# All attention scores issued 1.6 places sooner, with eighteen probability tiles instead of fourteen

## The chip, the cores and the metric

The kernel runs on one core of a Trainium2 chip. The metric is the device time of one execution in microseconds (us), the median of the runs. The engines are TensorE (PE, with its weight loads shown as PEld), VectorE (DVE), ScalarE (ACT), GpSimd (POOL) and SyncE (SP, which here only issues DMAs). Each engine works through its own list of instructions in order; semaphores tie the lists together.

## The reference

One transformer layer over 2 x 1024 tokens of width 512, in FP32, with 16 heads of 32:

```python
qkv = einsum('bsd,ed->bse', x, w_qkv) + b_qkv             # split into q, k, v, 16 heads
scores = q @ k^T / sqrt(32) + causal mask
attn = softmax(scores); out = attn @ v
x = layernorm(x + out @ w_out^T + b_out)
hidden = relu((x @ sign(up_w)^T) * up_scale)
x = layernorm(x + (hidden @ sign(down_w)^T) * down_scale * output_scale)
```

## The kernel before

Matmuls that need more precision than one pass gives are split into a high and a low part (`x_high`, `x_low` and so on). The order of all work is one list, made by `plan()` (L86): every piece of work is put at a *slot*, a number, and the list is sorted by slot, ties by the order of the calls. Every engine's block then walks this same list and issues what concerns it. So a slot decides only what stands before what, on each engine; it is no time.

Attention runs in 8 steps (`STEPS`), one for a batch element and a group of four heads. Step s covers the slots from 48s to 48s+48. Inside a step there are 48 *scores* (`NP`, L29): score n belongs to one half f of the queries (f=0 for n below 16), one tile j of 128 keys and one of the four heads h. A score is one matmul on PE (L1013), 512, 384, 256 or 256 columns wide for j on the diagonal (the last, 128 wide, is issued 256 wide) and 512 for the others. ACT takes its exponential out of PSUM into one of `RING` tiles of `probs` (L709), POOL masks the diagonal ones (L617). Score n of a step stands at slot n (L142).

What else stands in a step:

- `pv` (L1043) multiplies the four heads' probabilities of one tile j by v into `ps_heads`, `sum` (L1037) adds them up with ones into `ps_sum`. In steps 0 to 5 these groups go in pairs: groups 0 and 1 at slot 13, 2 and 3 at 19.6, 4 and 5 at 28, 6 and 7 at 36, 8 and 9 at 44, 10 and 11 at 52 (which is slot 4 of the next step), by `PAIRED` (L35). Steps 6 and 7 take them one by one (`ALONE`, L37). For groups 4 to 7 POOL first adds probabilities (L630), and `sum_added` (L1021, slot 43.9) sums those.
- `norm` (L824): after groups 0 to 3 (f=0), and again after 4 to 11 (f=1), DVE reads both banks, four times a reciprocal and a product into `heads_sb` (L833, L835). The next `pv` with j=0 waits for all four (L1028), since it writes into the same bank.
- `max` (L981, slots in `MAXIMA`, L42): 48 *units* of the next step's scores, whose row maxima DVE takes (L807, L811), and which become the shift of its softmax: `shift` (L992, ACT L694, DVE L821), at slots 36.02 and 51.9.
- `proj` (L945, slots in `BLOCK`, L46): the projections of q and k of later steps, with their evictions `full` and `high` on ACT (L682, L688).
- In step 6 `sign` and `split` on ACT and DVE (L715 to L745, L840) prepare late weights and fetched heads; in step 7 `attn` (L1061) is the output projection of the first 512 tokens, `std1` (L748) and `norm1` (L873) its layernorm, `turn` (L1070) its transposes. The FFN begins at slot 384.5 (`FIRST_UP`, L70; L1085, L1102).

Scores, units and shifts share five PSUM banks (four for the scores of step 7) in rotation, by `share()` (L229): each takes the bank used longest ago, and its matmul waits until ACT or DVE has read what lies there (`bank_read`, L916). An exponential also waits until the tile that it overwrites, `RING` scores back, was used (L705 to L708). Before the attention the `probs` tiles hold the first pieces of x (L444, L453).

Of the kernel before, what the change touches and what calls it, by code (L numbers as in the profile page):

```python
# [18 lines left out]
GH = P // HD  # L19
# [7 lines left out]

PIECES = [(f, j, h) for f in range(2) for j in range(4 * (f + 1)) for h in range(GH)]
NP = len(PIECES)  # L29
RING = 14  # L30
DIAG = [n for n, (f, j, h) in enumerate(PIECES) if j >= 4 * f]
ND = len(DIAG)


PAIRED = [13, 13, 19.6, 19.6, 28, 28, 36, 36, 44, 44, 52, 52]  # L35
# [16 lines left out]
FIRST_ADD, LAST_ADD = 4, 8  # L52
NA = 3 * GH
ADDING = STEPS - 2
# [31 lines left out]
def plan():  # L86
# [4 lines left out]
    def put(slot, what, s=0, n=0):  # L91
        todo.append((slot, len(todo), (what, s, n)))
# [39 lines left out]
        put(at + 6.5, "keep", 1, k)  # L132
        put((-104.5, -97)[k], "stack", 1, k)
    put(-104, "v_rows", 0)
    put(-1, "ones", 1)
    put(0.9, "row_max", 0, 1)
    put(1.2, "shift", 0, 1)

    for s in range(STEPS):
        t = NP * s  # L140
        for n in range(NP):
            put(t + n, "score", s, n)  # L142
        paired = s < STEPS - 2
        for g, at in enumerate(PAIRED if paired else ALONE[s % 2]):
            put(t + at, "pv", s, g)
            if g < FIRST_ADD or g >= LAST_ADD or s >= ADDING:
                put(t + at, "sum", s, g)
        if s < ADDING:
            for a in range(NA):
                put(t + 21.7 + 1.3 * a, "add", s, a)  # L150
            put(t + 43.9, "sum_added", s)
        for q, at in enumerate(PAIRED_NORM if paired else ALONE_NORM[s % 2]):
            put(t + at, "norm", s, q)
            if q % 4 == 3:
                put(t + at + 4.9, "store", s, q // 4)
        if s + 1 < STEPS:
            for u, at in enumerate(MAXIMA):
                put(t + at, "max", s + 1, u)
            put(t + 36.02, "shift", s + 1, 0)
            put(t + 47.2, "row_max", s + 1, 1)  # L160
            put(t + (51.9 if s + 2 < STEPS else 48.2), "shift", s + 1, 1)
            put(t + 17, "v_rows", s + 1)
        for ahead, k, at, each, evict, keep, fill in BLOCK if s < STEPS - 2 else LAST_BLOCK:
            if s + ahead < STEPS:
                for m in range(12):
                    put(t + at + each * m, "proj", s + ahead, 12 * k + m)
                put(t + evict, "full", s + ahead, k)
                put(t + evict + 0.05, "high", s + ahead, k)
                put(t + keep, "keep", s + ahead, k)
                put(t + fill, "stack", s + ahead, k)  # L170
# [30 lines left out]
    for i in range(CH):  # L201
        t = FIRST_UP + 16 * i
# [47 lines left out]
def build(nc, x_rows, x_cols, w_qk, w_v, b_qk, b_v, w_out, b_out, up_w, down_w, up_s, down_s, out_s, out):  # L250
    top = ExitStack()
    with top:
# [404 lines left out]
        def _(act):  # L657
# [4 lines left out]
            for what, s, n in todo:  # L662
# [33 lines left out]
                if what == "score":  # L696
                    _, width, _ = piece_cols(n)
                    off = P if width == P else 0
                    if s == 0 and n == 0:

                        act.wait_ge(s_xl[0], 8)
                        act.wait_ge(s_xl[1], 8)
                    act.wait_ge(s_score, NP * s + n + 1)

                    wait(act, s_pv, NP * s + n - RING + 1)  # L705
                    k = n - RING - GH * FIRST_ADD
                    if s < ADDING and 0 <= k < GH * (LAST_ADD - FIRST_ADD):
                        act.wait_ge(s_add, NA * s + (k if k < GH else k - GH) + 1)  # L708
                    nc.scalar.activation(probs[:, (NP * s + n) % RING, 0:width], bank(what, s, n)[:, off:off + width],  # L709
                                         ACT.Exp, scale=SCALE).then_inc(s_exp, 1)  # L710
                if what == "sign":
                    act.wait_ge(s_raw[n % 2], 16 * (n // 2 + 1))
                    src = raw[:, n % 2, :]
                    if n < 2:
                        nc.scalar.activation(wo[0][:, 2 * n:2 * n + 2, :].rearrange("p c e -> p (c e)"), src,  # L715
                                             ACT.Copy).then_inc(s_sign, 1)
                    elif n < 10:
                        if n == 6:

                            act.wait_ge(s_score, NP * (STEPS - 1))  # L720
                        k = (n - 2) % 4
                        nc.scalar.activation(up_sb[(n - 2) // 4][:, 2 * k:2 * k + 2, :, :].rearrange("p m c e -> p (m c e)"),
                                             src, ACT.Sign).then_inc(s_sign, 1)
                    else:
                        if n == 14:

                            act.wait_ge(s_pv, NP * STEPS)
                            act.wait_ge(s_st[1], 16 * STEPS)
                        if n == 10:

                            for k in range(NB):
                                act.wait_ge(s_stack[k], 48 * STEPS)
                            act.wait_ge(s_lo, NB * STEPS)
                        nc.scalar.activation(down_sb[:, 2 * (17 - n):2 * (18 - n), :].rearrange("p m e -> p (m e)"),
                                             src, ACT.Sign).then_inc(s_sign, 1)
# [416 lines left out]
```

## Time and profile before

| | us |
|---|---|
| median of 3 runs | 782.07 (779.53 to 782.5) |
| the profiled execution | 783.35, its span 781.6 |
| PE busy | 730.8 (94%) |
| DVE, ACT, POOL busy | 450.3, 317.0, 354.9 |
| mean granted TensorE clock | 0.979 |
| DMA queues | q1 and q10 hardware_dynamic, q8 and q14 instruction; no other |

PE is busy nearly throughout, so what can move is the little time in which it waits, and the stretches in which its clock is granted at half. The timeline rows read: start in us, duration in us, engine, line, operation, tiles written and read, partitions and columns, and how many instructions are merged (x). In brackets stands how long the engine was idle before, and what released it. Matmuls are pipelined: the distance from one start to the next is what one costs, and it is shorter than its duration.

### The profile page before, as it was taken

To read this page: it belongs to the slowest core of one execution; us is meant where nothing else is said; L and a number is where in the kernel's file an instruction comes from. 1 tells how busy PE (TensorE), PEld (TensorE's weight loads), DVE (VectorE), ACT (ScalarE), POOL (GpSimd) and SP (SyncE) were. 2 spreads that over 40 slices of the span, in tenths; PEclk is the share of its full clock that TensorE was granted. 3 is DMA by queue.
4 is the path that set the end of the run, shared out by engine and by line. 5 is a ranking of instruction groups with operands and counts; after the bars stand their busy time and mean duration, and the time that the engine had idled before them with its cause. 6 is when DMAs were issued, how large, how long until landed. Compare 5 with 4: busy or idle time off the path is not lost.

```text
span 781.6 us, 11689 instructions
## 1 busy us (share of the span) xinstructions
PE 730.8 (94%) x4032; PEld 508.9 (65%) x4032; DVE 450.3 (58%) x1086; ACT 317.0 (41%) x631; POOL 354.9 (45%) x487
## 2 busy tenths in 40 slices
PE   6899999999999999999978989999999999999993
PEld 4688665655656556565534543788778787878882
DVE  4176496785957859578566651632295429434515
ACT  5211355554655546565446556423222222221210
POOL 4461467394674947648322501542344235323333
PEclk9999999999999999999989899999999999999997
DMA  6965454435545354442577240403003101000101
GB/s 228 297 188 146 127 178 133 137 109 149 161 135 145 91 161 139 129 143 83 152 225 243 83 136 27 149 28 122 14 28 107 24 5 41 15 1 0 55 1 54
DMA packets 44619, 85.71 MB, mean 110 GB/s; under 512 B 4880, under 2 KB 13584, under 8 KB 44432
## 3 DMA queue, kind: packets, MB, share of 16 engines
q1 hardware_dynamic: 35536, 79.72, 33.8%
q10 hardware_dynamic: 9024, 5.24, 2.4%
q8 instruction: 32, 0.52, 0.3%
q14 instruction: 27, 0.22, 0.1%
HBM read 55.33 MB, written 29.36 MB: 108 GB/s over the span
## 4 chain that ended last, share of the span: by engine, by line
PE 70%; DVE 20%; issue 3%; DMA 3%; ACT 2%; POOL 1%; SPq 0%; ACTq 0%; DVEq 0%; POOLq 0%
PE ps_heads L1043 9%; PE ps_proj L1085 7%; DVE heads_sb L833 7%; PE ps_proj L945 6%; PE ps_score L1102 6%; PE ps_unit L1061 6%; DVE maxes L811 6%; PE ps_sum L1037 6%; PE ps_unit L1085 5%; PE ps_unit L981 4%; PE ps_heads L1102 3%; PE ps_sum L1102 3%; PE ps_unit L1013 3%; DVE heads_sb L835 2%; PE ps_score L981 2%
## 5 line engine op out<-in xcount | busy, mean ns | idle before, releaser
L653 POOL TENSOR_TENSOR hid_low<-hid_raw,hid_high 128x512 fp32r<-128x512 f32 x64 | 85.0, 1329 | 175.2 <-DVE hid_high L884 172.1
L709 ACT ACTIVATE probs<-ps_unit 128x512 f32<-128x512 f32 (+3 forms) x215 | 101.1, 491 | 91.7 <-PE ps_unit L1013 87.9
L617 POOL TENSOR_SCALAR_AFFINE_SELECT probs<-probs 128x128 f32<-128x128 f32 x256 | 73.3, 296 | 129.6 <-ACT probs L709 125.1
L709 ACT ACTIVATE probs<-ps_score 128x512 f32<-128x512 f32 (+3 forms) x156 | 75.1, 496 | 76.2 <-PE ps_score L1013 73.8
L807 DVE CUSTOM_DVE_ANT_0 ps_unit<-ps_unit,causal 128x256 f32<-128x256 f32 (+3 forms) x164 | 80.4, 509 | 41.2 <-PE ps_unit L981 40.3
L884 DVE CAST hid_high<-hid_raw 128x512 fp32r<-128x512 f32 x64 | 27.1, 424 | 127.2 <-ACT hid_raw L764 126.9
L981 PE MATMUL ps_unit<-stack 96*128 96x512 f32 (+3 forms) x247 | 86.0, 363 | 7.6 <-DVE maxes L807 3.8
L1043 PE MATMUL ps_heads<-probs,v_rows 128*32 128x512 f32 (+3 forms) x768 | 81.9, 504 | 10.1 <-DVE heads_sb L835 10.1
L1013 PE MATMUL ps_unit<-stack 98*128 98x512 f32 (+2 forms) x215 | 77.8, 368 | 3.9 <-DVE maxes L807 3.9
L611 POOL TENSOR_TENSOR parts<-qk_full,parts 128x512 fp32r<-128x512 f32 x32 | 41.1, 1284 | 58.2 <-ACT parts L688 58.0
L981 PEld LDWEIGHTS ps_unit<-stack 96*128 96x128 f32 x247 | 46.7, 193 | 31.6 <-DVE maxes L811 10.9
L833 DVE RECIPROCAL heads_sb<-ps_sum 128x128 f32<-128x128 f32 x64 | 60.8, 950 | 11.0 <-PE ps_sum L1037 11.0
L811 DVE TENSOR_REDUCE maxes<-ps_unit 128x1 f32<-128x512 f32 x83 | 54.3, 683 | 17.9 <-PE ps_unit L981 17.8
L630 POOL TENSOR_TENSOR added<-added,probs 128x512 f32<-128x512 f32 x48 | 60.9, 1282 | 0.0
L764 ACT ACTIVATE hid_raw<-ps_proj,up_scale 128x512 f32<-128x512 f32 x32 | 22.0, 689 | 93.6 <-PE ps_proj L1085 93.6
L1013 PE MATMUL ps_score<-stack 98*128 98x512 f32 (+2 forms) x156 | 57.2, 373 | 2.6 <-DVE h_even L789 1.5
L807 DVE CUSTOM_DVE_ANT_0 ps_score<-ps_score,causal 128x512 f32<-128x512 f32 (+3 forms) x92 | 46.1, 517 | 23.1 <-PE ps_score L981 22.8
L1037 PE MATMUL ps_sum<-probs,ones 128*32 128x512 f32 (+3 forms) x576 | 57.8, 467 | 0.0
L1013 PEld LDWEIGHTS ps_unit<-stack 98*128 98x128 f32 x215 | 41.0, 191 | 17.7 <-DVE maxes L807 4.3
L945 PE MATMUL ps_proj<-x_high,w_high 128*128 128x512 f32 x116 | 45.9, 422 | 6.7 <-ACT x_high L666 6.7
L1102 PE MATMUL ps_score<-down_sb,hid_high 128*128 128x512 f32 x124 | 50.1, 404 | 0.0
L981 PE MATMUL ps_score<-stack 96*128 96x512 f32 (+3 forms) x137 | 47.7, 362 | 1.6 <-DVE maxes L807 1.1
(195 smaller groups left out, 1456.7 us busy)
## 6 DMA issues: line engine op xcount, KB each, us to landing
stack<-qk_parts SPq DMA_DIRECT2D x96, 256.0 KB, 4.5
qk_parts<-parts SPq DMA_DIRECT2D x32, 512.0 KB, 2.8
v_all<-h_even ACTq DMA_DIRECT2D x16, 256.0 KB, 3.3
v_rows<-v_all SPq DMA_DIRECT2D x8, 512.0 KB, 4.6
heads_t<-heads_sb SPq DMA_DIRECT2D x16, 256.0 KB, 3.1
raw<-up_w SPq DMA_DIRECT2D x8, 512.0 KB, 3.5
x_tile<-x_rows SPq DMA_DIRECT2D x16, 256.0 KB, 5.0
raw<-down_w SPq DMA_DIRECT2D x8, 512.0 KB, 3.9
```

The lines of the kernel that those rows point to most:

```text
L653: nc.gpsimd.tensor_tensor(hid[1][:, (HM * s + n) % 3, :], hid_raw[:, n % 2, :], hid[0][:, (HM * s + n) % 3, :].bitcast(FP32), ALU.subtract ...
L709: nc.scalar.activation(probs[:, (NP * s + n) % RING, 0:width], bank(what, s, n)[:, off:off + width], ACT.Exp, scale=SCALE).then_inc(s_exp, 1)
L807: nc.vector.tensor_tensor_reduce(bank(what, s, n)[:, 0:width], bank(what, s, n)[:, 0:width], causal[:, HALF - width:], 1.0, NEG, ALU.add, ...
L811: nc.vector.tensor_reduce(maxes[:, 1, col:col + 1], bank(what, s, n)[:, :], AXIS_X, ALU.max).then_inc(s_max, 1)
L833: nc.vector.reciprocal(heads_sb[:, cols], ps_sum[:, cols]).then_inc(s_rc, 1)
L945: mm = nc.tensor.matmul(proj_bank(s, k)[:, :], ws[wp][:, c, t, :], xs[xp][:, c, t0:t0 + HALF], start=(m == 0), stop=(m == 11))
L981: nc.tensor.matmul(bank(what, s, n)[:, 0:width], stack[s % 2][0:96, 1, f, h, i % 4 * P:(i % 4 + 1) * P], stack[s % 2][0:96, 0, c, h, 0:wid ...
L1013: nc.tensor.matmul(bank(what, s, n)[:, 0:width + off], stack[s % 2][0:98, 0, j // 4, h, j % 4 * P:(j % 4 + 1) * P], stack[s % 2][0:98, 1, ...
L1037: nc.tensor.matmul(ps_sum[rows, at:at + width], ones[:, :], tile, **args).then_inc(s_pv, 1)
L1043: mm = nc.tensor.matmul(ps_heads[rows, at:at + width], v_rows[:, s % 2, j, rows], tile, **args)
L1085: mm = nc.tensor.matmul(ps_up[n % 2][:, :], up_sb[n // 8][:, n % 8, m % DC, :], turned[s % 2][m // DC][:, m % DC, :], start=(m == 0), stop ...
L1102: mm = nc.tensor.matmul(ps_down[i][:, :], hid[part][:, (HM * s + n) % 3, i * P:(i + 1) * P], down_sb[:, down_at(n), :], start=(n == 0 and ...
```

## The change

Three things. The scores (and with them their exponentials and masks, which are issued at the same entry of the list) are put at slot n - 1.6 instead of n; nothing else is moved except `ones` of step 1, which has to stay ahead. The ring of `probs` grows from 14 to 18 tiles. The room for it (4 x 2 KB a partition) comes from the scratch memory of software-driven DMAs, cut to 1024 bytes, which also lets two more of the late weights' pieces be written before the last probabilities are used (`n == 16`). The wait of an exponential for POOL's additions is written so that it also holds across steps.

```diff
-RING = 14
+RING = 18
+LEAD = 1.6
...
-    put(-1, "ones", 1)
+    put(-1 - LEAD, "ones", 1)
...
         for n in range(NP):
-            put(t + n, "score", s, n)
+            put(t + n - LEAD, "score", s, n)
...
                     wait(act, s_pv, NP * s + n - RING + 1)
-                    k = n - RING - GH * FIRST_ADD
-                    if s < ADDING and 0 <= k < GH * (LAST_ADD - FIRST_ADD):
-                        act.wait_ge(s_add, NA * s + (k if k < GH else k - GH) + 1)
+                    s0, k = (NP * s + n - RING) // NP, (n - RING) % NP - GH * FIRST_ADD
+                    if 0 <= s0 < ADDING and 0 <= k < GH * (LAST_ADD - FIRST_ADD):
+                        act.wait_ge(s_add, NA * s0 + (k if k < GH else k - GH) + 1)
...
-                        if n == 14:
+                        if n == 16:
...
-    nc = bacc.Bacc("TRN2", target_bir_lowering=False, num_devices=1)
+    nc = bacc.Bacc("TRN2", target_bir_lowering=False, num_devices=1, dynamic_dma_scratch_size=1024)
```

Below, lines of the changed kernel are two higher than those of before (from L135 on).

**PE, across the end of step 1.** These are the last groups of step 1 (L1043 and L1037, 256 and 128 columns), and the scores of step 2 around them (L1013, 384 columns wide for n = 4 to 7), with projections (L945) between. Before:

```order
L992 MATMUL ps_unit<-ident,row_max 16x128
L1043 MATMUL ps_heads<-probs,v_rows 32x256 x4
L1037 MATMUL ps_sum<-probs,ones 32x256 x4
L1043 MATMUL ps_heads<-probs,v_rows 32x128 x4
L1037 MATMUL ps_sum<-probs,ones 32x128 x4
L1013 MATMUL ps_unit<-stack 128x384
L945 MATMUL ps_proj<-x_low,w_high 128x512
L1013 MATMUL ps_unit<-stack 128x384
L945 MATMUL ps_proj<-x_low,w_high 128x512
L1013 MATMUL ps_score<-stack 128x384
L945 MATMUL ps_proj<-x_low,w_high 128x512
L1013 MATMUL ps_score<-stack 128x384
```

After:

```order
L1015 MATMUL ps_unit<-stack 128x384
L947 MATMUL ps_proj<-x_high,w_high 128x512
L1015 MATMUL ps_unit<-stack 128x384
L947 MATMUL ps_proj<-x_high,w_high 128x512
L994 MATMUL ps_unit<-ident,row_max 16x128
L1045 MATMUL ps_heads<-probs,v_rows 32x256 x4
L1039 MATMUL ps_sum<-probs,ones 32x256 x4
L1045 MATMUL ps_heads<-probs,v_rows 32x128 x4
L1039 MATMUL ps_sum<-probs,ones 32x128 x4
L1015 MATMUL ps_score<-stack 128x384
L947 MATMUL ps_proj<-x_low,w_high 128x512
L1015 MATMUL ps_score<-stack 128x384
```

Before, the four scores of 384 columns all follow the groups; after, two of them stand ahead of the groups and of the shift (L992, L994 after), and two behind. Between these groups and the next (slot 13) PE has 10 scores before and 9 after, beside the same units and projections. From the groups at slot 19.6 to those at 28 it has 9 before and 8 after.

**PE, at slot 43.9 of step 1.** L1021 is the sum of the added tiles, L1043 the first group of the pair at 44, L1013 a score. Before:

```order
L1013 MATMUL ps_unit<-stack 128x256
L981 MATMUL ps_unit<-stack 128x384
L1021 MATMUL ps_sum<-added,ones 32x512 x4
L1013 MATMUL ps_unit<-stack 128x256
L1043 MATMUL ps_heads<-probs,v_rows 32x512 x4
L1037 MATMUL ps_sum<-probs,ones 32x512 x4
```

After:

```order
L1015 MATMUL ps_unit<-stack 128x256
L983 MATMUL ps_score<-stack 128x384
L1023 MATMUL ps_sum<-added,ones 32x512 x4
L1045 MATMUL ps_heads<-probs,v_rows 32x512 x4
L1039 MATMUL ps_sum<-probs,ones 32x512 x4
```

The lone score between the sum and the pair has moved ahead of both.

**ACT, at slot 22.5 of step 7.** The table loads stand around the standard deviation (L748, L750 after), the exponentials are L709 (L711 after), L754 (L756 after) copies the first transpose. The tile names are the banks in their rotation of four. Before:

```order
L709 ACTIVATE probs<-ps_unit2 128x512
L709 ACTIVATE probs<-ps_score0 128x512
L748 ACT_TABLE_LOAD
L748 ACTIVATE std1<-mom1,eps 128x4
L709 ACT_TABLE_LOAD
L709 ACTIVATE probs<-ps_proj 128x512
L709 ACTIVATE probs<-ps_score1 128x512
L709 ACTIVATE probs<-ps_unit2 128x512
L709 ACTIVATE probs<-ps_score0 128x512
L754 ACTIVATE t_even_high<-ps_unit1 128x4x128
```

After:

```order
L711 ACTIVATE probs<-ps_proj 128x512
L711 ACTIVATE probs<-ps_score0 128x512
L750 ACT_TABLE_LOAD
L750 ACTIVATE std1<-mom1,eps 128x4
L711 ACT_TABLE_LOAD
L711 ACTIVATE probs<-ps_score1 128x512
L711 ACTIVATE probs<-ps_unit2 128x512
L711 ACTIVATE probs<-ps_proj 128x512
L756 ACTIVATE t_even_high<-ps_unit1 128x4x128
```

Before, scores 23 to 26 follow the table loads and the copy of the first transpose comes behind four of them; after, scores 23 and 24 are done ahead, and the copy comes behind three (25 to 27).

## Rows read from the trace of the kernel before

**Rows 1.** windows view (busy time by stretch); columns in its first line

```profile
core 0: us, PE busy (x) PEld busy (x) DVE busy (x) ACT busy (x) POOL busy (x), PEclk, DMA share, GB/s
88.50:401.00 312.50, 296.93 (x2011) 185.97 (x2011) 224.04 (x634) 173.05 (x375) 190.66 (x319) 1.00 0.48 138
401.00:489.40 88.40, 78.55 (x476) 38.35 (x476) 42.52 (x97) 51.53 (x99) 23.70 (x53) 0.90 0.40 126
```

**Rows 2.** the same view, around the stretches at the lower clock

```profile
397.80:401.20 3.40, 0.15 (x1) 0.00 (x0) 3.30 (x7) 1.04 (x2) 0.24 (x1) 1.00 0.67 271
401.20:408.00 6.80, 6.16 (x21) 2.22 (x22) 1.23 (x5) 2.69 (x5) 2.35 (x1) 0.50 0.64 154
435.40:442.20 6.80, 6.38 (x35) 3.67 (x27) 1.26 (x5) 2.94 (x6) 3.60 (x7) 0.50 0.02 5
466.10:469.50 3.40, 1.43 (x7) 0.79 (x6) 1.64 (x4) 3.36 (x7) 0.00 (x0) 1.00 0.00 0
469.50:472.90 3.40, 3.40 (x17) 0.60 (x16) 1.15 (x2) 2.06 (x5) 0.00 (x0) 0.50 0.00 0
```

**Rows 3.** line 1043 (heads matmuls), idle before it: us, times

```profile
  DVE heads_sb L835: 24.4, 26
  POOL probs L617: 3.5, 9
```

**Rows 4.** timeline of PE around two waits for the normalization (before and in step 3)

```profile
238.54 0.28 PE L1013 MATMUL ps_score<-stack 98*128 98x256 f32 x1
239.76 0.64 PE L1043 MATMUL ps_heads<-probs,v_rows 128*32 128x512 f32 x4 [0.95 <-DVE heads_sb L835]
...
254.76 0.40 PE L945 MATMUL ps_proj<-x_low,w_high 128*128 128x512 f32 x1
255.00 0.39 PE L1013 MATMUL ps_unit<-stack 98*128 98x512 f32 x1
255.81 0.64 PE L1043 MATMUL ps_heads<-probs,v_rows 128*32 128x512 f32 x4 [0.42 <-DVE heads_sb L835]
```

**Rows 5.** timeline of DVE, first and last of one normalization

```profile
234.86 0.96 DVE L833 RECIPROCAL heads_sb<-ps_sum 128x128 f32<-128x128 f32 x1 [0.75 <-PE ps_sum L1037]
...
239.41 0.29 DVE L835 TENSOR_TENSOR heads_sb<-ps_heads,heads_sb 128x128 f32<-128x128 f32 x1
```

**Rows 6.** timeline of PE around the sum of the added tiles (step 2)

```profile
224.13 0.28 PE L1013 MATMUL ps_unit<-stack 98*128 98x256 f32 x1
224.25 0.34 PE L981 MATMUL ps_unit<-stack 96*128 96x384 f32 x1
...
225.51 0.38 PE L1013 MATMUL ps_score<-stack 98*128 98x256 f32 x1
225.83 0.64 PE L1043 MATMUL ps_heads<-probs,v_rows 128*32 128x512 f32 x4
```

**Rows 7.** timeline of PE, step 6, after the first normalization

```profile
401.84 1.65 PE L1013 MATMUL ps_unit<-stack 98*128 98x512 f32 x3 [3.88 <-DVE maxes L807]
```

**Rows 8.** timeline of ACT, DVE and PE, step 6, the second split

```profile
427.32 0.62 ACT L745 ACTIVATE t_even_high<-h_even 128x512 fp32r<-128x512 f32 x1
427.98 0.69 DVE L840 TENSOR_TENSOR t_even_low<-h_even,t_even_high 128x512 fp32r<-128x512 f32 x1 [0.89 <-ACT t_even_high L745]
...
429.13 0.33 PE L981 MATMUL ps_unit<-stack 96*128 96x128 f32 x1 [1.26 <-DVE maxes L807]
```

**Rows 9.** timeline of ACT and PE, step 7, after the standard deviation

```profile
466.73 1.28 ACT L709 ACT_TABLE_LOAD   x1
468.76 0.47 PE L1013 MATMUL ps_proj<-stack 98*128 98x512 f32 x1 [0.55 <-ACT probs L709]
469.62 1.08 PE L1043 MATMUL ps_heads<-probs,v_rows 128*32 128x512 f32 x4
```

**Rows 10.** timeline of PE, last score and first matmul of the FFN

```profile
488.65 0.38 PE L1013 MATMUL ps_proj<-stack 98*128 98x256 f32 x1
489.44 0.47 PE L1085 MATMUL ps_proj<-t_even_high,up_a 128*128 128x512 f32 x1 [0.41 <-issue]
```

## The prediction

> **What bounds the kernel now.** I read first the busy time by stretch: through steps 0 to 5 of the attention PE is busy 296.93 of 312.50 us at a full clock of 1.00, through the rest of the attention 78.55 of 88.40 at 0.90 [rows 1]. So PE bounds the kernel, and only its idle time and its clock can change, since the edit removes and adds no work. Then what PE's idle time ends on, line by line: before the heads matmuls it is 24.4 us in 26 entries (13 waits, each seen once by the matmuls and once by their weight loads) for the normalization on DVE, against 3.5 us for masked probabilities [rows 3]. The timeline gives one wait of each kind: 238.54 to 239.76 is 1.22 us for a score that costs 0.12, and 255.00 to 255.81 is 0.81 us for one that costs 0.24 [rows 4, 6]. One normalization takes DVE from 234.86 to 239.41 + 0.29 = 239.70, 4.84 us, whatever PE does beside it, and PE's next group starts 0.06 us after its end [rows 4, 5]. Last the clock by stretch: three pieces of 6.80, 6.80 and 3.40 us run at 0.50, that is 1.2 of 2.4 GHz, all in steps 6 and 7; ahead of the first PE was busy 0.15 of 3.40 us, ahead of the third 1.43 of 3.40 [rows 2].
>
> **The change, part by part.** Prices are start-to-start distances: 0.24 us for 512 columns (254.76 to 255.00, [rows 4]), 0.12 for 256 (224.13 to 224.25, [rows 6]), 0.18 for 384 between them.
>
> *The waits for the normalization, steps 0 to 5 and the starts of 6 and 7.* Between the groups that end a half and those that need `ps_heads` free, PE has scores, units and projections to do beside DVE's 4.84 us. After slot 52 it had scores 4 to 13 (four of 384 columns, six issued with 256), now 6 to 14: 0.18 + 0.18 - 0.12 = 0.24 us of cover less. From 19.6 to 28 it had nine of 512 columns, now eight: 0.24 less. The end of these stretches is set by DVE, so each becomes not shorter but idler, and the score that left is done where PE is busy: from 13 to 19.6 (scores 14 to 19 become 15 to 21) and from 44 to 52. There are six waits of the first kind that bind (before steps 1 to 6), six of the second, and one in step 7 from 17.5 to 24 (seven scores become six). 13 x 0.24 = **+3.1 us**.
>
> *From 28 to 36* DVE's row maxima pace PE; a score of 512 columns is replaced there by one of 384, which saves nothing, since DVE sets the end: 6 x 0.06 = **+0.3**.
>
> *The lone score at slot 43.9*, between the sum of the added tiles and the pair of groups, costs 225.51 to 225.83, 0.32 us, and 0.12 in a row of its like [rows 6]. It moves ahead of both: 6 x 0.20 = **-1.2**.
>
> *Step 6, normalization at 18.4.* Two units stand behind it on DVE, so PE runs out of banks for 3.88 us, then does three scores in 1.65 us before the next group [rows 7]. Afterwards it gets two scores further before it stops, and two instead of three follow the release. The group starts with the release of DVE plus two: **-0.5** (1.65/3 at the half clock, 0.24 at the full one).
>
> *Step 6, the second split.* ACT's half at 427.32 stands behind the exponential of score 40, which in turn waits for a matmul behind group 8 (slot 39.5). DVE's half waits 0.89 us for it, and PE then waits 1.26 us for a bank [rows 8]. Now scores 40 and 41 are ahead of the group. ACT still has a conversion of weights and two exponentials to do ahead, so I take only part of the 0.89: **-0.7**, between 0 and -1.26.
>
> *Step 7, the standard deviation.* ACT loads a table for the square root and one back (1.28 us, [rows 9]); the exponentials of 23 and 24 wait behind. PE therefore waits 0.55 us at 468.76 and does two scores before the group at 469.62. Now 23 and 24 are ahead of the tables, score 28 finds its bank free, and only 29 waits until about 468.76: the group starts one score sooner, **-0.4** (469.62 - 468.76, halved). Two turns later PE waits for ACT's and DVE's copies of a transpose, with two scores as cover in place of three: **+0.2**.
>
> *End of the attention.* The FFN's first matmul needs the bank of score 47, issued right before it: 488.65 to 489.44, 0.79 us where 0.12 are work [rows 10]. With score 47 ahead of group 10 its exponential is long done: **-0.7**.
>
> *What costs nothing.* The larger ring only takes a wait away: with 14 tiles, exponential 14 (now at slot 12.4) would need the tile that group 0 gives back at slot 13; with 18, number 18 does, at slot 16.4. ACT's evictions at 13.05, 19.65 and 44.05 now have one or two exponentials more ahead of them; the groups of heads and sums that stand there on PE cover that. If they did not, the projection behind would start up to 0.62 us later (a 512-column copy on ACT, [rows 8]), in stretches at whose end PE idles anyway. ACT's copy of the shift at 51.9 has two more exponentials ahead; the normalization behind it on DVE had been idle 0.75 us before its start [rows 5], and that takes it up. On SP no entry passes another; its DMAs for stacks and parts hang on units and projections, which keep their places. POOL's masks pass some additions of steps 0 to 5, whose sum is taken 8 slots after the last of them. The smaller scratch serves software-driven DMAs, and no queue here is one.
>
> Sum: 3.1 + 0.3 - 1.2 - 0.5 - 0.7 - 0.4 + 0.2 - 0.7 = **+0.1 us**. On the profiled execution's 783.35 that is 783.4; it stood 1.3 above the median, so I forecast 782.07 + 0.1 = 782.2.
>
> **What the clock does** is not in this sum, and its bounds are wide. In the three half-clock pieces PE is busy 6.16 + 6.38 + 3.40 = 15.94 us [rows 2]; if none came, 8.0 us would be saved. One more like the first would cost 6.16/2 = 3.1. I take no change, since the idle stretch of 3.88 us ahead of the first shrinks only to about 3.6.
>
> In steps 0 to 5 PE idles about 1.1 us at a time ([rows 4]: 1.22 - 0.12) and the clock stays at 1.00 [rows 1]. The Trainium skill, in "TensorE: Matmul & The Clock Gate", section "A second HAM failure mode: psum-queue depth-cycling", says that short idles between groups of matmuls that cycle through PSUM banks make the clock swing between its two levels, each swing costing throughput. This kernel is of that kind; its trace disagrees at 1.1 us of idleness, and at 3.88 us it agrees. By the rule the longer waits cost what rival 2 gives, by the rows nothing beyond the sum.
>
> **Rivals.**
> 1. *The clock stays up.* The change shortens the idleness ahead of the half-clock pieces: 0.55 us in step 7 [rows 2, 9], some 0.7 in step 6 a few us before 435.40 [rows 8]. If the last two pieces vanish: (6.38 + 3.40)/2 = 4.9 us, so 782.2 - 4.9 = 777.3; all three, 774.2. Against it: of the 3.40 - 1.43 = 1.97 us of idleness ahead of the third only 0.55 go.
> 2. *The clock falls in the early steps*, the slower side. The waits at a step's start grow from 1.1 to 1.34 us. If that is enough for a fall, each costs up to 3.1 us. From two on the kernel is slower: 782.2 + 6.2 = 788.4; with all six, about 801. Against it: rows at 1.00 throughout, and the step up is only 0.24.
> 3. *Only the lost cover shows.* The savings in steps 6 and 7 hang on chains over three engines; if they all come to nothing, 782.07 + 3.1 + 0.3 - 1.2 + 0.2 = 784.5, and without the lone score's 785.7.
> 4. *The lead does not arrive*: if PE's banks, not the order, hold the scores back, they are executed where they were, and the time is 782.1.
>
> **Chances.** Forecast 0.40, rival 1 0.20, rival 2 0.12, rival 3 0.18, rival 4 0.10. A measurement of this kernel can tell 0.5% from no change, 3.9 us. Faster than 778.2: rival 1, and 0.02 of the rest, 0.22. Slower than 786.0: rival 2, and 0.05 of rival 3 with a bad wait on top, 0.17. Same: 0.61. The forecast's own range is 780 to 784.5 from the bounds of the split and the step 6 terms; the range given, 776.8 to 786.8, takes in most of rivals 1 and 3 and leaves out the clock's far ends.
>
> **What would show it.** Right: the waits before the pair at slot 13 grow to about 1.46 us from the last score's start, those before slot 28 to 1.05; the distance from the pair at 13 to the pair at 28 grows from 16.05 us (239.76 to 255.81, [rows 4]) by 0.34, the score and a half more ahead of slot 19.6; no score stands between the sum and the pair at 44; the FFN's first matmul follows without an idle. Wrong: if steps 1 to 5 get shorter, the stretches that I took as paced by PE had slack; if the granted clock of steps 6 and 7 is far from 0.90, the time is the clock's and not the sum's.

## The result, and the profile after

The changed kernel takes 775.69 us (median of 19 runs, 773.07 to 779.61), the kernel before 780.25 (19 runs on the same chips, 777.48 to 782.5). The ratio is 0.9947, with a 95% interval of 0.9934 to 0.996: 4.1 us faster. The forecast was 782.2, no change, with a range of 776.8 to 786.8. It stood on 782.07, the median of three runs; the nineteen give 780.25, so 1.8 us of the distance are the base's and not the change's. The profiled execution took 774.34 us, its span is 772.6 (before 781.6), at a mean granted clock of 0.991 (before 0.979).

The page of the changed kernel, span and busy times, then the clock in 40 slices (tenths of 2.4 GHz):

```profile
span 772.6 us, 11683 instructions
...
PE 722.7 (94%) x4032; PEld 505.2 (65%) x4032; DVE 450.5 (58%) x1086; ACT 317.2 (41%) x631; POOL 354.4 (46%) x487
...
PEclk9999999999999999999999999999999999999998
```

PE is busy 8.1 us less with the same 4032 matmuls: 722.7 against 730.8. Nearly all of it is clock: in the half-clock pieces of the two profiles (the one in the start-up, shown below, among them) PE is busy 22.26 us before and 6.66 after, and half of the difference is 7.8. Busy time by stretch, as in [rows 1], and then around the clock's steps, as in [rows 2]:

```profile
85.40:398.00 312.60, 296.55 (x2013) 186.32 (x2013) 223.34 (x633) 174.92 (x377) 190.27 (x319) 1.00 0.48 138
398.00:480.40 82.40, 72.96 (x474) 35.63 (x474) 43.35 (x99) 49.76 (x97) 23.33 (x53) 0.96 0.42 135
396.70:400.10 3.40, 0.32 (x1) 0.19 (x1) 3.33 (x8) 0.27 (x1) 0.00 (x0) 1.00 0.48 175
400.10:403.50 3.40, 3.26 (x14) 0.89 (x17) 0.28 (x2) 2.03 (x3) 1.55 (x1) 0.50 1.06 246
428.80:432.20 3.40, 2.35 (x20) 1.01 (x20) 2.32 (x11) 1.19 (x2) 1.58 (x3) 1.00 0.31 110
432.20:435.60 3.40, 3.26 (x28) 2.43 (x29) 1.00 (x3) 2.56 (x5) 3.31 (x5) 1.00 0.04 7
458.20:461.60 3.40, 1.76 (x8) 0.97 (x8) 1.64 (x4) 3.36 (x5) 0.00 (x0) 1.00 0.00 0
461.60:465.00 3.40, 3.40 (x17) 0.60 (x16) 1.15 (x2) 2.17 (x5) 0.00 (x0) 0.50 0.00 0
```

Steps 0 to 5 take about as long as before (312.60 us for 312.50, both at 1.00; from their first group to group 4 of step 6, 0.6 us more). Steps 6 and 7 take 82.40 for 88.40. The half-clock piece at 435.40 of [rows 2] has no counterpart: at 432.20 the clock stays at 1.00. The first piece is 3.40 us long instead of 6.80. The third is unchanged.

Part of the 9.0 us between the two spans is no gain of the change. The FFN begins 8.99 us earlier, but 2.8 of these are there already at the first group of step 0: before, the clock fell at 36.00 us in the start-up, behind this stretch of PE (kernel before, windows):

```profile
32.50:36.00 3.50, 1.45 (x7) 0.83 (x5) 0.00 (x0) 0.00 (x0) 1.12 (x1) 1.00 1.10 304
36.00:42.80 6.80, 6.32 (x16) 5.19 (x17) 2.99 (x10) 1.15 (x2) 2.52 (x2) 0.50 1.09 349
```

and after, it did not, behind nearly the same (the changed kernel):

```profile
32.50:36.00 3.50, 1.48 (x7) 0.86 (x5) 0.00 (x0) 0.00 (x0) 1.16 (x1) 1.00 1.08 308
36.00:42.80 6.80, 6.59 (x31) 5.56 (x32) 4.89 (x17) 2.31 (x4) 3.63 (x3) 1.00 1.09 346
```

Among the profiles of the kernels below whose start-up is that of before, three show such a piece, 3.4 us long (1, 6 and 7 of the list), and the others don't. The first group starts at 94.52 us in the profile of before, at 91.9 to 92.3 in those three and at 90.1 to 91.1 in the others. Two profiles, then, differ by 1 to 4 us that is chance. So I use two measures from here on: distances inside a profile for what the order does, and for the clock the half-clock time of a run, 2 x (1 - granted clock) x span, averaged over the runs of a kernel. It is 19.9 us for the changed kernel (13.9 to 28.0) and 27.5 to 29.8 for the kernel before in the different sets of runs. In every profile 7 to 9 us of it lie at the very end, where PE has no work left, so only the differences count. Among runs of one kernel, 1 us more of it goes with 0.33 to 0.39 us (before) or 0.35 us (after) more time; this is an association among runs, no experiment.

Where the order tells, by distances in the profiles (after less before): from the pair at slot 13 to that at 28 in step 3, +0.38; from the pair at 36 to that at 44, -0.30 to -0.38 in each early step; from 44 to the next 52, +0.04; all in all 0.6 us more from step 0 to step 5, about 0.1 a step. From group 4 of step 6 to the start of step 7, 39.18 us for 44.56: -5.4. From there to group 10 of step 7, -0.5, and from group 10 to the FFN, -0.9.

### The profile page after: what moved, and what is told of

Its sections match the earlier page's. It is cut to its first block, busy times and chain, and to the rows that moved or that the text cites. A ratio compares the mean times of both kernels' runs of the same rounds, so it can differ in the third digit from the quotient of the medians.

```text
span 772.6 us, 11683 instructions
## 1 busy us (share of the span) xinstructions
PE 722.7 (94%) x4032; PEld 505.2 (65%) x4032; DVE 450.5 (58%) x1086; ACT 317.2 (41%) x631; POOL 354.4 (46%) x487
## 4 chain that ended last, share of the span: by engine, by line
PE 71%; DVE 19%; issue 3%; DMA 3%; POOL 2%; ACT 2%; SPq 0%; ACTq 0%; POOLq 0%
PE ps_heads L1045 9%; PE ps_proj L1087 7%; DVE heads_sb L835 7%; PE ps_proj L947 7%; PE ps_score L1104 6%; PE ps_unit L1063 6%; PE ps_unit L1087 5%; PE ps_sum L1039 5%; DVE maxes L813 5%; PE ps_unit L983 4%; PE ps_heads L1104 3%; PE ps_unit L1015 3%; PE ps_sum L1104 3%; PE ps_score L1015 2%; PE ps_score L983 2%
## 5 line engine op out<-in xcount | busy, mean ns | idle before, releaser
L711 ACT ACTIVATE probs<-ps_unit 128x512 f32<-128x512 f32 (+3 forms) x216 | 101.9, 490 | 88.4 <-PE ps_unit L1015 85.0
L711 ACT ACTIVATE probs<-ps_score 128x512 f32<-128x512 f32 (+3 forms) x155 | 75.2, 498 | 77.0 <-PE ps_score L1015 75.6
L809 DVE CUSTOM_DVE_ANT_0 ps_unit<-ps_unit,causal 128x512 f32<-128x512 f32 (+3 forms) x162 | 80.1, 511 | 32.5 <-PE ps_unit L983 31.5
L1045 PE MATMUL ps_heads<-probs,v_rows 128*32 128x512 f32 (+3 forms) x768 | 80.3, 502 | 11.8 <-DVE heads_sb L837 11.8
L983 PE MATMUL ps_unit<-stack 96*128 96x512 f32 (+3 forms) x246 | 83.8, 354 | 5.7 <-DVE maxes L809 2.5
L1039 PE MATMUL ps_sum<-probs,ones 128*32 128x512 f32 (+3 forms) x576 | 55.5, 457 | 0.0
L1045 PEld LDWEIGHTS ps_heads<-probs,v_rows 128*32 128x32 f32 x768 | 19.5, 109 | 47.8 <-issue 23.6
```

What stands on the lines that cost most here:

```text
L809: nc.vector.tensor_tensor_reduce(bank(what, s, n)[:, 0:width], bank(what, s, n)[:, 0:width], causal[:, HALF - width:], 1.0, NEG, ALU.add, ...
L983: nc.tensor.matmul(bank(what, s, n)[:, 0:width], stack[s % 2][0:96, 1, f, h, i % 4 * P:(i % 4 + 1) * P], stack[s % 2][0:96, 0, c, h, 0:wid ...
L1039: nc.tensor.matmul(ps_sum[rows, at:at + width], ones[:, :], tile, **args).then_inc(s_pv, 1)
L1045: mm = nc.tensor.matmul(ps_heads[rows, at:at + width], v_rows[:, s % 2, j, rows], tile, **args)
```

## The experiments

Three explanations stood against each other: the clock (less idleness in step 6, so less time at half clock; the lead's own waits about nothing), the waits (the edit's savings are larger than priced, wherever they lie, at the same clock), and the ring of 18 tiles with its smaller scratch. Each kernel was timed against the kernel before on the same chip, in three sets: kernels 1 to 4 in one, 5, 6, 7 and 9 in the next, 8 and 10 to 12 in the last. The half-clock time of the kernel before is 27.5, 28.1 and 29.8 us in these sets. Half-clock time is the mean per run, as defined above. Where a difference of two ratios is given, "give or take" comes from their two intervals.

| | median, us (runs) | ratio to before, 95% | half-clock, us |
|---|---|---|---|
| changed kernel | 775.69 (19) | 0.9947 [0.9934, 0.9960] | 19.9 |
| 1. ring alone | 780.63 (12) | 1.0008 [0.9993, 1.0022] | 30.0 |
| 2. lead in steps 0 to 5 | 782.37 (12) | 1.0028 [1.0009, 1.0046] | 28.9 |
| 3. lead in steps 6 and 7 | 774.66 (6) | 0.9933 [0.9914, 0.9952] | 18.6 |
| 4. lead in step 7 | 779.50 (12) | 0.9986 [0.9972, 1.0000] | 27.9 |
| 5. lead in step 6 | 776.49 (7) | 0.9951 [0.9933, 0.9969] | 20.8 |
| 6. before + fillers | 777.09 (7) | 0.9955 [0.9939, 0.9971] | 14.6 |
| 7. steps 6, 7 + fillers | 775.04 (6) | 0.9916 [0.9889, 0.9942] | 13.9 |
| 8. changed + fillers | 773.93 (6) | 0.9903 [0.9875, 0.9930] | 13.4 |
| 9. split moved | 778.76 (12) | 0.9983 [0.9971, 0.9996] | 26.2 |
| 10. lone score moved | 779.03 (12) | 0.9981 [0.9963, 0.9999] | 28.9 |
| 11. steps 6, 7 + lone score | 772.08 (6) | 0.9890 [0.9856, 0.9925] | 17.5 |
| 12. all of it | 769.82 (6) | 0.9854 [0.9828, 0.9881] | 10.5 |

**1. The ring alone.** The changed kernel, with the lead at 0:

```diff
+LEADS = [0.0] * 8
...
-            put(t + n - LEAD, "score", s, n)
+            put(t + n - LEADS[s], "score", s, n)
```

> Ring of 18, small scratch, but every score at its old slot (lead 0): the order on every engine is that of before. Theory A (the order of the scores makes the gain): same time as before, ratio 0.999 to 1.001, and the first half-clock stretch at 36 us comes and goes as in before. Rival (the ring or the moved buffers make part of the gain, at the start, where the changed kernel's profile reaches the first score 3.1 us sooner): ratio 0.996 to 0.997.

1.0008 [0.9993, 1.0022]: the ring and the smaller scratch show no gain by themselves (by the interval at most 0.6 us). The gain is the order's.

**2. The lead in steps 0 to 5 only.** `LEADS = [LEAD] * 6 + [0.0] * 2`.

> The lead of 1.6 in steps 0 to 5 only, steps 6 and 7 at their old slots. Theory A (gain sits in steps 6 and 7; early steps cost 0.1 us each): ratio 1.000 to 1.002, the start of group 4 of step 5 0.6 us later than before once the start-up is taken off. Rival (the early steps or the start-up gain): ratio below 0.998.

1.0028 [1.0009, 1.0046], 2.2 us slower (0.7 to 3.6), more than expected. The early part costs, as the waits for the normalization said it would.

**3. The lead in steps 6 and 7 only**, rising over the first two scores of step 6:

```diff
+            put(t + n - (0 if s < 6 else min(LEAD, 0.8 * n) if s == 6 else LEAD), "score", s, n)
```

> The lead in steps 6 and 7 only. Theory A: the whole gain or a little more, ratio 0.993 to 0.995 (4 to 5 us), with fewer or shorter half-clock stretches between 400 and 475 us. Rival (gain is in the early part): ratio above 0.998.

0.9933 [0.9914, 0.9952], as expected: the whole gain, and the half-clock time goes from 27.5 to 18.6 us. So it lies late.

**4. The lead in step 7 only** (the same line with 7 for 6).

> The lead in step 7 only. Theory A with the sizes of the two profiles (step 6, from group 4 to the next step's group 0, gave 5.4 us of which much is clock; step 7 from group 4 on 1.7): ratio 0.998 (1.1 to 1.7 us faster). Rival (step 7 carries the gain): ratio 0.995.

0.9986 [0.9972, 1.0000], 1.1 us, at an unchanged half-clock time (27.9 for 27.5).

**5. The lead in step 6 only** (rising at its start, falling again over the first scores of step 7).

> The lead in step 6 only, taken back over the first scores of step 7. From the lead in 6 and 7 (0.9933) and in 7 alone (0.9986): ratio 0.994 to 0.996 if the two add up; half-clock time a run 7 to 9 us less than before. My sum had 1.2 us for step 6 at an unchanged clock: 0.9985 if the clock played no part.

0.9951 [0.9933, 0.9969], as expected: 3.8 us of the gain come with step 6, and with them the clock (20.8 us for 28.1).

**6. Fillers in the kernel before.** The order is the one of before. Added are 24 matmuls of 512 columns whose result is thrown away, into `ps_proj`, which is free there: 14 where PE runs out of banks [rows 7], and 5 twice near the second split [rows 8].

```diff
+        for at, count in [(21.5, 14), (42.05, 5), (46.04, 5)]:
+            for m in range(count):
+                put(late + at, "fill", 0, m)
...
+                if what == "fill":
+                    pe.wait_ge(s_qk, NB * STEPS)
+                    nc.tensor.matmul(ps_proj[:, :], stack[0][0:98, 0, 0, 0, 0:P], stack[0][0:98, 1, 0, 0, :], start=True, stop=True)
```

> The kernel before with 24 matmuls of 512 columns added in step 6, into the idle ps_proj bank, whose results are thrown away: 14 where PE waits 3.88 us for DVE behind the normalization, 5 and 5 where it waits 1.26 and 1.2 us for a bank. Theory C (part of the gain is clock: idle PE ahead of 401 and 435 us gives the half-clock stretches): both stretches vanish, half-clock time a run falls by 8 to 13 us, ratio 0.994 to 0.996. Rival W (only the waits count, the clock is an accident beside it): the waits' ends stay where DVE and ACT set them, and the added work costs or changes nothing, ratio 1.000 to 1.002.

0.9955 [0.9939, 0.9971], as theory C expected: 3.5 us faster with more work and nothing else. The timeline of PE of this kernel, where [rows 7] have 3.88 us of idleness and three scores in 1.65 us (L1116 are the fillers, L1016 scores):

```profile
395.06 3.36 PE L1116 MATMUL ps_proj<-stack 98*128 98x512 f32 x14
399.12 1.15 PE L1016 MATMUL ps_unit<-stack 98*128 98x512 f32 x3 [0.70 <-DVE maxes L810]
400.20 1.07 PE L1046 MATMUL ps_heads<-probs,v_rows 128*32 128x512 f32 x8
```

From the first of the three scores to the group are 1.08 us now, 1.58 before (401.84 to 403.42), and the windows of the same kernel show why, and that of the pieces in steps 6 and 7 only the last is left:

```profile
395.00:398.40 3.40, 3.40 (x15) 2.47 (x14) 3.30 (x6) 1.09 (x2) 0.32 (x1) 1.00 0.67 271
398.40:401.80 3.40, 2.70 (x20) 0.90 (x19) 1.31 (x5) 2.14 (x4) 0.04 (x1) 1.00 0.75 174
435.40:442.00 6.60, 6.60 (x49) 5.01 (x42) 5.94 (x10) 5.44 (x11) 4.62 (x11) 1.00 0.38 121
463.40:466.80 3.40, 3.40 (x19) 1.04 (x12) 1.14 (x2) 1.53 (x4) 0.00 (x0) 0.50 0.00 0
```

The half-clock time falls by 13.5 us (28.1 to 14.6), the time by 3.5, or 0.26 us for each. In "TensorE: Matmul & The Clock Gate", section "HAM oscillation — how this bites in real kernels", the Trainium skill counts half of the throttled time as lost. Here it is less. That a slow PE runs into waits that it would have had anyway would explain it, but no run here separates that.

**7. Fillers in kernel 3**: 13 at slot 22.0 and 5 at 45.6 of step 6.

> The lead in steps 6 and 7 only (774.7 us, 0.9933), and 18 such matmuls: 13 in the wait behind step 6's normalization, 5 in the one before group 10. Theory C: 1 to 2 us faster than with the lead alone, ratio 0.990 to 0.992, no half-clock stretch at 397 to 401 us. Rival W: ratio 0.993 to 0.995.

0.9916 [0.9889, 0.9942]: inside the expected ratio, but 1.3 us below kernel 3, give or take 2.5, so the clock's part in kernel 3 does not stand out of the noise. Its profile still has a half-clock piece of 3.4 us behind the fillers, at 401.6, where theory C expected none; the half-clock time is 13.9 us, near kernel 6's 14.6. At this level of the clock, kernel 6's mean of 776.93 us becomes 773.79: 3.1 us, give or take 2.4, are the late lead's own.

**8. Fillers in the changed kernel**, the same 18.

> The changed kernel with 18 thrown-away matmuls in step 6, as in the kernel with the late lead (0.9916). The difference between the two is the price of the lead in steps 0 to 5 with the clock of step 6 levelled. By my sum's waits and the traces' other terms 0.6 to 2 us: ratio 0.9925 to 0.9945. Rival (the early lead costs nothing): 0.9916 again.

0.9903 [0.9875, 0.9930], faster than expected; the rival's 0.9916 lies inside the interval. Against kernel 7, from which it differs only by the lead of steps 0 to 5 (and the chip), it is 1.0 us faster, give or take 3.0: too wide to contradict kernel 2, which had that lead cost 2.2 us (0.7 to 3.6). The traces have a price too: 0.6 us from the first group on, and the first group itself starts at 91.7 to 91.8 us in the three profiles with the early lead (changed, 2, 8), at 90.1 to 91.1 in the seven that have neither it nor the piece in the start-up, about 1.1 us more.

This kernel against kernel 6 is the whole change with fillers on both sides: 0.9903 for 0.9955, 4.1 us, give or take 2.5, at nearly the same half-clock time (13.4 and 14.6). The change gains as much between these two as without fillers.

**9. The second split alone**, ahead of the group in the kernel before:

```diff
-        put(late + 38 + 2 * i, "split", 0, i)
+        put(late + (39.49 if i == 1 else 38 + 2 * i), "split", 0, i)
```

> The kernel before, but ACT's half of the second split (slot 40) stands ahead of the exponential of score 40, at 39.49; every score keeps its place. My term of the sum for it: 0.7 us, so ratio 0.9985 to 0.9995, DVE's wait of 0.89 us before its half gone. Rival (the clock amplifies it, since the idle ahead of the stretch at 435 us shrinks below what starts it): ratio 0.995 to 0.997 with that stretch gone. Rival (other waits take its place): 1.000.

0.9983 [0.9971, 0.9996], 1.3 us, where 0.7 was expected. DVE's half no longer waits, and of PE's 1.26 us [rows 8] stay 0.21 (timelines of DVE and PE):

```profile
423.02 0.69 DVE L840 TENSOR_TENSOR t_even_low<-h_even,t_even_high 128x512 fp32r<-128x512 f32 x1
...
424.17 0.33 PE L981 MATMUL ps_unit<-stack 96*128 96x128 f32 x1 [0.21 <-DVE maxes L807]
```

But the half-clock piece behind it stays. Windows of this kernel, then of kernels 5 and 3:

```profile
426.80:430.20 3.40, 2.09 (x16) 1.30 (x19) 2.85 (x10) 1.24 (x4) 2.31 (x4) 1.00 0.45 154
430.20:437.00 6.80, 6.38 (x35) 3.73 (x31) 1.50 (x6) 2.61 (x6) 3.38 (x7) 0.51 0.02 5
```

```profile
426.80:430.20 3.40, 2.26 (x21) 1.05 (x20) 2.72 (x11) 1.12 (x4) 1.30 (x5) 1.00 0.52 161
430.20:437.00 6.80, 4.70 (x34) 3.38 (x35) 3.95 (x7) 3.16 (x6) 5.49 (x7) 1.00 0.02 4
```

```profile
426.80:430.20 3.40, 2.09 (x20) 1.03 (x20) 2.62 (x11) 1.34 (x4) 1.30 (x4) 1.00 0.48 157
```

At 430.20 the clock is 0.51 in kernel 9 and 1.00 in kernel 5, and it stays up in kernel 3 too. PE's busy time ahead is 2.09 us in kernel 9, where it falls, and 2.26 and 2.09 where it doesn't: these rows do not tell which. What the runs say is that the split alone takes little half-clock time away (26.2 us for 28.1), and step 6's whole lead much (20.8).

**10. The lone score alone.** In the kernel before, score 44 of steps 0 to 5 ahead of the sum:

```diff
+            put(t + n - (0.15 if n == 44 and s < ADDING else 0), "score", s, n)
```

> The kernel before, with one edit: in steps 0 to 5 score 44 stands at 43.85, ahead of the sum of the added tiles (43.9), so that no lone score is left between that sum and the pair at 44. My price was 0.20 us a step; the two traces have 0.31 (8.76 us from the pair at 36 to the pair at 44 became 8.44). Expected 1.2 to 2.0 us less, ratio 0.9975 to 0.9985. Rival (the time is given back at the next wait): 1.000.

0.9981 [0.9963, 0.9999], 1.5 us, as expected. The timeline of PE in step 2, to be read against [rows 6] (their first entries are the same score and unit):

```profile
219.93 0.28 PE L1013 MATMUL ps_unit<-stack 98*128 98x256 f32 x1
220.05 0.34 PE L981 MATMUL ps_unit<-stack 96*128 96x384 f32 x1
220.23 0.28 PE L1013 MATMUL ps_score<-stack 98*128 98x256 f32 x1
220.44 1.07 PE L1021 MATMUL ps_sum<-added,ones 128*32 128x512 f32 x8
221.32 1.04 PE L1043 MATMUL ps_heads<-probs,v_rows 128*32 128x512 f32 x8
```

From the first score to the pair are 1.39 us, before 225.83 - 224.13 = 1.70: 0.31 a step. The score saves its 0.20, and the sum itself gets 0.1 shorter with the pair right behind it (0.88 from start to start).

**11. The late lead with the lone score** (kernels 3 and 10 together).

> The lead of 1.6 in steps 6 and 7 only (0.9933), and score 44 of steps 0 to 5 at 43.85. If the parts add up: 1.2 to 2.0 us below the late lead alone, ratio 0.991 to 0.992, and faster than the changed kernel (0.9947) by about 2 us. Rival (the early lead was worth its place): 0.994 or more.

0.9890 [0.9856, 0.9925]: faster than the changed kernel, whose interval begins at 0.9934, and a little more than the parts together. Its step 6 has the order of kernel 3, yet its profile shows a half-clock piece where those of kernels 3 and 5 have none:

```profile
423.40:426.80 3.40, 2.25 (x22) 1.10 (x21) 2.93 (x11) 1.41 (x4) 1.28 (x4) 0.99 0.49 161
426.80:433.60 6.80, 6.17 (x31) 3.67 (x28) 1.40 (x5) 3.00 (x5) 4.75 (x7) 0.50 0.01 2
```

PE was busy 2.25 us ahead of it, 2.26 in kernel 5, where the clock stays up. So in a single profile this piece is partly chance, and only the half-clock time of many runs tells (17.5 us here, for 29.8).

**12. All of it**: kernel 11, with 19 fillers in step 6 (14 at 22.0, 5 at 45.6) and 10 in step 7, into a bank free there:

```diff
+        for at, count in [(23.9, 5), (25.9, 5)]:
+            for m in range(count):
+                put(last + at, "fill", 1, m)
```

> Late lead, score 44 at 43.85, the 19 fillers of step 6, and 10 more in step 7 (five ahead of group 4, where PE waits 1.4 us for the normalization, five ahead of the first transpose, where it waits 1.4 us for the layernorm). Theory C: the half-clock stretch near 462 us goes too, ratio 0.986 to 0.989, the fastest. Rival W (idle time was free to fill, its clock worth nothing): as with the lead and score 44 alone, 0.991 to 0.992.

0.9854 [0.9828, 0.9881], 11.4 us faster than before, a little beyond the expected 0.986, and the fastest of all. Its window of steps 6 and 7:

```profile
395.00:474.00 79.00, 74.00 (x492) 38.63 (x494) 43.68 (x100) 49.25 (x95) 23.19 (x52) 1.00 0.43 138
```

They take 79.00 us at a clock of 1.00, where [rows 1] have 88.40 at 0.90. The half-clock piece of step 7 is gone, but the profiles of kernels 2 and 8 lack it too, without fillers there. The runs tell more: 10.5 us of half-clock time, of which 7 to 9 lie at the very end, for 17.5 in kernel 11.

## Why the prediction was wrong

The step that failed is the term of the clock: "I take no change, since the idle stretch of 3.88 us ahead of the first shrinks only to about 3.6." A run of the changed kernel has 19.9 us of half-clock time, one of the kernel before 27.5 to 29.8. The stretch itself did not even shrink. PE in step 6 of the changed kernel, as in [rows 7]:

```profile
395.20 0.62 PE L1015 MATMUL ps_unit<-stack 98*128 98x512 f32 x2
399.78 0.51 PE L1015 MATMUL ps_unit<-stack 98*128 98x512 f32 x1 [3.96 <-DVE maxes L809]
...
401.15 1.94 PE L1045 MATMUL ps_heads<-probs,v_rows 128*32 128x512 f32 x8
```

It idles 3.96 us and the clock still falls there, if for 3.40 us only. But the text argued from one of three pieces. The one at 435.40 goes, which was the core of rival 1, held at 0.20; the piece of step 7, which rival 1 counted on too, stays. The text also put all half-clock pieces of the trace into steps 6 and 7, and left out the one in the start-up. Its own sign of being wrong came true: the clock of steps 6 and 7 is 0.96 and not 0.90.

How much of the gain is clock, three readings tell. Over the runs, 7.6 to 9.9 us less half-clock time, at 0.35 each, would be 2.7 to 3.5 of the 4.1 us. The second reading is the stretch from group 4 of step 6 to group 0 of step 7, in the kernel before, the changed kernel, kernel 6 and kernel 8 (the kernel before and the changed one, with 24 and 18 fillers):

```profile
403.42:447.98 44.56, 40.08 (x220) 20.51 (x219) 26.02 (x64) 25.81 (x49) 17.65 (x32) 0.87 0.52 164
401.15:440.33 39.18, 36.29 (x220) 18.43 (x219) 25.86 (x64) 25.03 (x49) 17.77 (x33) 0.97 0.56 180
400.20:441.36 41.16, 37.47 (x230) 20.07 (x229) 27.08 (x64) 25.86 (x50) 17.60 (x32) 1.00 0.55 176
401.06:439.24 38.18, 36.10 (x226) 19.03 (x225) 25.87 (x64) 25.54 (x50) 17.76 (x33) 1.00 0.59 187
```

At full clock on both sides the stretch still gets 3.0 us shorter, so of the 5.4 us some 2.4 are clock and 3.0 the order's own, if the fillers themselves cost nothing. (Half of the difference in busy time at half clock, 12.54 us [rows 2] to 3.26, would make 4.6: too much.) The third are the times of kernels 8 and 6: with nearly the same half-clock time on both sides the change is worth 4.1 us, give or take 2.5, as much as without fillers. So the clock's share of the 4.1 us lies between nothing and some 3.5 us; the runs do not settle it, and the savings in step 6 beside the clock were priced too low as well (below).

That half-clock time costs, and that idle time in step 6 brings it, kernel 6 shows: it keeps the order and fills the idleness. That the lead of step 6 takes half-clock time away, the means of kernels 3, 5 and 4 show (18.6, 20.8, 27.9). In single profiles there is chance in it. With step 6 in the order of before and no fillers, the clock falls between 425 and 438 us in all six (6.8 us in before, 1 and 9, 13.6 in 4 and 10, twice 3.4 in 2); with the lead in step 6 it does so in one of four (kernel 11, not 3, 5 and the changed kernel). What is not shown is what decides it, behind much the same busy time.

The other terms:

- *Waits for the normalization, +3.1.* The cover is lost as foretold: the distance from pair 13 to pair 28 grows by 0.38 (forecast 0.34), to 253.71 - 237.28 = 16.43. PE in the changed kernel, as in [rows 4]:

```profile
235.56 0.34 PE L983 MATMUL ps_unit<-stack 96*128 96x384 f32 x1
237.28 1.07 PE L1045 MATMUL ps_heads<-probs,v_rows 128*32 128x512 f32 x8 [1.39 <-DVE heads_sb L837]
...
252.91 0.39 PE L947 MATMUL ps_proj<-x_low,w_high 128*128 128x512 f32 x1
253.71 1.06 PE L1045 MATMUL ps_heads<-probs,v_rows 128*32 128x512 f32 x8 [0.41 <-DVE heads_sb L837]
```

  The first wait's idle time grows from 0.95 to 1.39 us (from the last matmul's start 1.72, forecast 1.46); the second keeps its 0.41, since a projection stands last ahead of it now (from the matmul in front of that, 252.67, it is 1.04 us, about the 1.05 forecast from the last score). And the idle time by line, as in [rows 3]:

```profile
  DVE heads_sb L837: 28.3, 26
```

  That is 3.9 us more in 26 entries, of which half are weight loads. The page of each kernel has PE's own 13 waits: 10.1 us before, 11.8 after, 1.7 us more where 3.1 was forecast. The part on the second half of a step was wrong: the distance from the pair at 44 to the next at 52 grows by 0.04, not 0.24.
- *28 to 36, +0.3.* 0.06 a step, as forecast.
- *Lone score, -1.2.* Undersized: 0.31 a step, 1.9 in all (kernel 10). The changed kernel has it too: 223.32 - 222.05 = 1.27 us for 1.70, less the 0.12 of the score that is no longer in that row.

```profile
222.05 0.28 PE L1015 MATMUL ps_score<-stack 98*128 98x256 f32 x1
222.17 0.34 PE L983 MATMUL ps_score<-stack 96*128 96x384 f32 x1
222.44 1.06 PE L1023 MATMUL ps_sum<-added,ones 128*32 128x512 f32 x8
223.32 1.04 PE L1045 MATMUL ps_heads<-probs,v_rows 128*32 128x512 f32 x8
```

  With these three, steps 0 to 5 come to +0.1 a step in the traces instead of +0.3 (3.1 x 12/13 + 0.3 - 1.2 = 2.0, over six).
- *Step 6, normalization at 18.4, -0.5.* Oversized: from the release of PE to the group are 401.15 - 399.78 = 1.37 us, before 403.42 - 401.84 = 1.58. The second score now waits too (it starts 0.65 us behind the first).
- *Second split, -0.7.* Undersized. DVE's half follows its predecessor without a wait (0.89 before [rows 8]); PE's wait falls by 0.88, and moving the split alone is worth 1.3 us (0.3 to 2.3). It was the only term for the stretch above, which got 3.0 us shorter at full clock.

```profile
423.11 0.69 DVE L842 TENSOR_TENSOR t_even_low<-h_even,t_even_high 128x512 fp32r<-128x512 f32 x1
...
424.25 0.33 PE L983 MATMUL ps_unit<-stack 96*128 96x128 f32 x1 [0.38 <-DVE maxes L809]
```

- *Step 7, -0.4 and +0.2; end of the attention, -0.7.* About right: from the first transpose to the next group 461.95 - 460.26 = 1.69 us for 469.62 - 467.55 = 2.07, and PE's wait two turns later grows from 0.8 to 1.1. In all -0.5 up to group 10 and -0.9 from there on in the trace; kernel 4 has both at 1.1 us. The FFN's first matmul now starts behind the groups and not behind a score, but its idle time stays: 0.37 us for 0.41 [rows 10], so "without an idle" did not come true.

```profile
480.45 0.93 PE L1087 MATMUL ps_proj<-t_even_high,up_a 128*128 128x512 f32 x3 [0.37 <-issue]
```

- *No cost of ring and scratch.* Right (kernel 1).

Of the rivals, 1 (777.3 on the old base, 4.8 us faster) is the nearest in time and half right in mechanism. The clock in the early steps (2) did not fall: 1.00 in all 312.6 us, with waits of 1.39 us in them. The Trainium skill's rule on short idles between groups that cycle through PSUM banks ("TensorE: Matmul & The Clock Gate", section "A second HAM failure mode: psum-queue depth-cycling") is thus not borne out in those steps. In step 6 the clock does swing, but there single waits are up to 3.96 us long. Rival 3, only the lost cover, describes kernel 2 (2.2 us slower; 2.0 by its terms for those steps), not the whole. Rival 4 is out: the order arrives, as the four rows of step 2 show.

So the 4.2 us between the sum (+0.1) and the result (-4.1) are the clock's and the waits' of step 6, both to the same side, in shares that stay open. With the clock levelled by fillers (kernels 6 and 7) the late lead is worth 3.1 us, give or take 2.4, where the forecast's terms for steps 6 and 7 make 1.9 with the wait in step 7 counted (0.24 - 0.5 - 0.7 - 0.4 + 0.2 - 0.7). The early lead costs: 2.2 us in kernel 2 (0.7 to 3.6), some 1.5 in the traces, of which the forecast had none at the first group.

## What to carry to other kernels

Where a trace shows pieces at half clock, price every one of them apart by the idle time ahead of it, and ask of each edit nearby whether it adds or takes some. A gap that can't be closed can be filled: matmuls that are thrown away, in a bank that is free, made the kernel before 3.5 us faster and none of the others measurably slower (7, 8, 12), and on both sides of a comparison they test how much of a gain is the clock's; that test needs more than six runs a kernel to tell 2 us. An edit on everything is best split by stage before it is kept: here one part cost, one paid, and the paying part with one score of the other beat both kernels.

## What was unexpected of the hardware

- 24 superfluous matmuls of 512 columns make the kernel 3.5 us faster.
- A single matmul of 256 columns between two groups of 32-column tiles costs 0.31 us more than the 0.12 that is its pace in a row: 0.20 for itself and 0.1 for the group ahead of it, which takes 0.88 us from start to start when the next group follows, and 0.99 when a single score does (225.51 less 224.52 in the trace of before).
- The clock's fall comes and goes between profiles behind nearly the same work: in the start-up at 1.45 and 1.48 us of busy PE in the 3.50 ahead, in step 6 at 2.25 and 2.26 in the 3.40 ahead. What tips it is not visible in these rows.
